# Two filler matmuls of 512 columns ahead of each product of the node network's chunks

## What is computed

```python
h = maximum(layernorm(x), 0)
# layer 0: edge network, sum over a node's edges, node network
e = relu(concat([edge_attr, h[src], h[dst]]) @ We1 + be1)
e_new = relu(e @ We2 + be2) @ We3 + be3
agg = segment_sum(e_new, dst)
g = relu(concat([h, agg]) @ Wn1 + bn1)
g = relu(g @ Wn2 + bn2)
x = x + g @ Wn3 + bn3
h = maximum(layernorm(x), 0)
# layer 1: attention-like weights over 8 heads, weighted sum, 8 products
x = x + layer1(h, src, dst, edge_weight, var_u, var_c, var_w, var_b)
```

## Time and profile before

| | |
|---|---|
| median of three runs | 2298.4 us |
| the profiled execution, its own time | 2296.56 us |
| its span, first to last instruction | 2294.8 us |
| mean granted TensorE clock, share of full | 0.698 |
| PE busy | 1689.2 us (74%) |
| POOL busy | 1626.8 us (71%) |
| DVE busy | 1346.8 us (59%) |
| ACT busy | 848.5 us (37%) |

### The profile page before, as it was taken

How to read it: one execution, slowest core, us unless ns; L and a number is a source line. 1 busy time by engine, 2 the same in 40 slices (tenths; PEclk the granted TensorE clock), 3 DMA queues, 4 the chain that set the end, 5 groups by cost and what they waited for, 6 DMA issues and landing times.

```text
span 2294.8 us, 54235 instructions
## 1 busy us (share of the span) xinstructions
PE 1689.2 (74%) x9941; PEld 1179.9 (51%) x9941; DVE 1346.8 (59%) x5883; ACT 848.5 (37%) x2528; POOL 1626.8 (71%) x1700
## 2 busy tenths in 40 slices
PE   4798999999899988999946656656556565655565
PEld 3455555555555555555435545544445454444454
DVE  6344443434444444344247777777777777777776
ACT  1333333333333333333224444444344434343432
POOL 3777777777777777777437777777777777777773
PEclk7789988989999899898655555555555555555555
DMA  2544444444444444444133333333333333333332
GB/s 75 122 100 102 93 97 96 103 92 101 101 98 96 95 101 99 93 100 97 37 92 99 98 97 97 95 97 94 98 95 97 95 96 96 97 95 96 96 96 60
DMA packets 353333, 216.99 MB, mean 95 GB/s; under 512 B 284830, under 2 KB 325881, under 8 KB 353056
## 3 DMA queue, kind: packets, MB, share of 16 engines
q0 software_dynamic: 66800, 113.26, 21.5%
q1 hardware_dynamic: 284822, 102.20, 18.6%
q10 hardware_dynamic: 1684, 1.24, 0.2%
HBM read 209.80 MB, written 6.69 MB: 94 GB/s over the span
## 4 chain that ended last, share of the span: by engine, by line
issue 24%; DVE 23%; PE 19%; POOL 15%; DVEq 9%; DMA 6%; ACT 3%; POOLq 0%; SPq 0%; ACTq 0%
POOL X L602 15%; DVEq L1246 6%; DMA X<-table_src,slot_s 4%; PE bank L1408 4%; DVE EQW L1187 3%; PE bank L1391 3%; PE bank L1417 3%; ACT EX L831 2%; DVE EX L1227 2%; PE bank L1399 2%; DVE r L1219 2%; DVE r L1210 2%; DVE L L1205 2%; DVE r L1214 2%; DVE r L1223 2%
## 5 line engine op out<-in xcount | busy, mean ns | idle before, releaser
L610 POOL DMA_INDIRECT G<-table_node_and_list,slot_s x825 | 798.6, 968 | 317.0 <-issue 250.7
L602 POOL DMA_INDIRECT X<-table_src,slot_s x825 | 788.5, 956 | 290.7 <-issue 270.3
L1519 PE MATMUL bank<-Q,G 125*64 125x128 f32 x1650 | 419.8, 427 | 398.6 <-DVE Q L1240 398.6
L1519 PEld LDWEIGHTS bank<-Q,G 125*64 125x64 f32 x1650 | 316.7, 223 | 416.9 <-DVE Q L1240 268.1
L1391 PE MATMUL bank<-filler 128*128 128x384 bf16 x1100 | 380.7, 346 | 2.4 <-issue 2.4
L1045 DVE TENSOR_TENSOR sT<-sT,bank 65x16 f32 x275 | 46.2, 168 | 554.0 <-PE bank L1427 523.0
L831 ACT ACTIVATE EX<-L 125x24 f32<-125x24 f32 x275 | 61.2, 223 | 611.2 <-DVE L L1205 597.8
L1408 PE MATMUL bank<-XT,w_ex 128*64 128x375 f32 x550 | 257.4, 553 | 4.2 <-issue 4.2
L763 ACT COPY XT<-bank 128x375 f32<-128x375 f32 x275 | 129.9, 472 | 328.0 <-PE bank L1399 317.5
L1417 PEld LDWEIGHTS bank<-w,H 65*125 65x125 f32 x1650 | 235.2, 202 | 0.0
L1417 PE MATMUL bank<-w,H 65*125 65x64 f32 x1650 | 224.3, 275 | 0.0
(11 more groups left out here) (168 smaller groups left out, 2270.5 us busy)
## 6 DMA issues: line engine op xcount, KB each, us to landing
KBT<-in_dst SPq DMA_DIRECT2D x550, 70.3 KB
X<-in_edge_attr SPq DMA_DIRECT2D x275, 93.8 KB
HK<-keys SPq DMA_DIRECT2D x275, 93.8 KB
X<-table_src,slot_s POOLq DMA_INDIRECT x825
G<-table_node_and_list,slot_s POOLq DMA_INDIRECT x825
BW<-table_dst_parts SPq DMA_DIRECT2D x275, 6.0 KB
UW<-table_logit_src_parts SPq DMA_DIRECT2D x275, 0.8 KB
table_node_and_list<-sm SPq DMA_DIRECT2D x1, 1562.5 KB
```

Source lines behind the costliest of these rows:

```text
L602: pool.indirect_dma_start(X[:, j, q, D:2 * D], None, tA, bass.IndirectOffsetOnAxis(ap=slot_s[:, j, q:q + 1], axis=0)).then_inc(gat_a[0][j] ...
L610: pool.indirect_dma_start(G[:, j, q, :], None, tH, bass.IndirectOffsetOnAxis(ap=slot_s[:, j, q:q + 1], axis=0)).then_inc(g_gather[j], 16)
L1519: last = pe.matmul(bank[2 + j % 2][0:D, 0:WM], G[0:P, j, q, 0:D], Q[:, j % 2, q].rearrange("p m n -> p (m n)"), start=(q == 0), stop=(q == ...
```

## The change

`filler` grows from 384 to 512 columns, `fill` gets a column count that stage 0 leaves at 384, and in the node network two fillers of 512 columns stand ahead of each of g1, g2 and x1, behind the waits of that product and in its bank: 7 chunks x 3 kinds x 2 = 42 matmuls.

```diff
-        filler = sb("filler", [128, 384], BF16)
+        filler = sb("filler", [128, 512], BF16)
...
-            def fill(to):
+            def fill(to, n=384):

-                pe.matmul(to[:, 0:384], filler[:, 0:128], filler[:], start=True, stop=True)
+                pe.matmul(to[:, 0:n], filler[:, 0:128], filler[:, 0:n], start=True, stop=True)
...
                     if c >= 2:
                         done_act(pe, ("g1", c - 2))
+                    for _ in range(2):
+                        fill(bank[c % 2], 512)
                     pe.matmul(bank[c % 2][0:D, 0:hi - lo], wn1h[:], hT[:, lo:hi], start=True, stop=False)
...
                     done_act(pe, ("g1", c))
                     if c >= 2:
                         done_act(pe, ("g2", c - 2))
+                    for _ in range(2):
+                        fill(bank[2 + c % 2], 512)
                     pe.matmul(bank[2 + c % 2][0:D, 0:hi - lo], wn2[:], hT[:, lo:hi], start=True, stop=True
...
                     done_act(pe, ("g2", c))
                     if c >= 2:
                         done_dve(pe, ("x1", c - 2))
+                    for _ in range(2):
+                        fill(bank[4 + c % 2], 512)
                     for n, b in enumerate(chunk_blocks(c)):
```

## The result

The changed kernel takes 2316.14 us (median of 8 runs, 2312.04 to 2317.84) beside 2299.03 us before (8 runs): a ratio of 1.0072, 95% interval 1.0057 to 1.0088. It is 17 us slower. The profiled execution took 2317.82 us, 21.3 more than the one of before; 3.4 of these lie ahead of the network, which stage 0 reached at 1108.14 in place of 1104.73, and that is the scatter of stage 0 from run to run (one and the same kernel, profiled twice as e2 and e9, reached the network at 1104.2 and at 1110.3).

The account below looks back on a forecast made before the run. The prediction took the node network, PE bound at half clock, as what the change could affect. Its terms, -4.2 + 0.5 - 0.8 = -4.5 us, led to 2293 us, own range 2286 to 2298, whole range 2285 to 2319.

Parts of the forecast that it names:

- What bounds the kernel: Node network between the edge loops: PE bound at half clock, PE's gains or losses up to the first half's logits reach the end.
- Which clock: Node network: clock falls at about 1106 us, returns about as late as in stage 0, 9.6 us; gain 4.2 us.
- rival A: Clock stays at half through the network, whose products use 65 rows; fillers all cost, 21.3 us, so 2318; chance 0.25.
- A pair: Two fillers ahead of a network product, with its change of weights: 1.05 us at half clock, 0.6 at full.
- The chunk with fillers at full clock: One chunk of the node network, three products with their filler pairs: 5.5 us at full clock.
- the path up to chunk 3: Network's start to third product of chunk 3: 29.1 us at full clock, 53.4 at half with fillers, 37.7 before.
- break-even: Node network: the change neither gains nor loses if full clock returns 19 us after the network's start.
- The lists: List loads ahead of the table write: about 1.7 us later, 5 us of cover, the bound only for gains above 9 us.
- The layer norm of the first half: On DVE behind the third product of chunk 3: takes 7.3 us whatever PE does, so faster PE gains nothing there.
- The other term: Products with w_u behind the network, already partly at full clock: counted 0, bounds -1 to +1 us.
- The fall at the start: Clock falls to half at about 1106 us, as before, when it fell after 1.2 us of the network.
- Rival B: Clock never falls, as the first filler pair follows the gap at once: gain 8.9 us, 2288 to 2289; chance 0.07.

Follow-up runs that it names:

- e2: The changed kernel plus seven 512-column fillers in the idle time ahead of the network: 2289.80 us profiled, four others 2308.43 to 2313.65; ratio to before 1.0065.
- e9: The kernel of e2 unchanged, profiled once more: 2309.16 us.
- e8: The changed kernel with six fillers over 65 rows, in place of two over 128, ahead of each network product: 2349.22 us, ratio to before 1.0229.
- e6: The changed kernel, two fillers kept, with the network's products over 128 rows in place of 65: 2298.16 us, ratio to before 0.9999.
- e4: The kernel before with the network's products over 128 rows in place of 65, no fillers in the network: 2290.00 us, ratio 0.9964.
- e3: The kernel before plus seven 512-column fillers in the idle time ahead of the network, none in the network: 2296.93 us, ratio 0.9997.
- e11: The kernel of e7 with g1's second matmul reading sT in order, not every 25th element (wrong result, same work): 2288.49 us, one execution.
- e7: The kernel before with network products over 128 rows and seven fillers in the idle time ahead, none in the network: 2288.55 us, ratio 0.9965.
- e1: The changed kernel with six 512-column fillers in place of two ahead of each network product: 2311.31 us, ratio to before 1.0058.
- e10: The changed kernel with four fillers per product in place of two, and seven in the idle time ahead of the network: 2300.17 us, ratio to before 1.0022.
- e5: The changed kernel with four fillers in place of two ahead of each network product: 2333.55 us, ratio to before 1.0156.
- e12: The kernel of e7 with the degree products one product earlier, behind the first chunk's g1: 2286.83 us, ratio to before 0.9959.

## Why the prediction failed

**What bounds the kernel: right.** The network is on the chain, PE bound, and what is lost there arrives at the end: 17.7 us from the network's start to the table write, 17 us in the kernel. Both loops and the table's DMA are as they were.

**The step that failed: "Which clock".** The forecast counted on a return to full clock within some 10 us "about as late as in stage 0", because the fillers' share of the time is the same there and here. It stayed at 0.50 for all of the 61.4 us. The forecast took the fillers for the whole of the difference between the two streams. What the rest of the stream is made of differs as well: stage 0's transposes and window sums use 125 rows and its first product 128, beside smaller ones, while the network's products use 65. e8 and e6 show that this decides: six fillers over 65 rows leave the clock down where six over 128 lift it, and the same two fillers come with 1.00 after 6 us once the products use 128 rows. The rival A had named this reason and was given 0.25; it was the case. That the measured time lies inside the stated range is owed to that rival, for which the range was widened, and not to the forecast. The row for it was in the trace of before, read for another purpose: a PE busy for 44.31 of 45.10 us at 0.50 says that these products do not lift the clock even when PE is busy 98% of the time, and stage 0 is no measure for a stream of them. The Trainium skill asks in general for TensorE to be kept busy (TensorE: Matmul & The Clock Gate, "Why this matters for your kernels"); e4 agrees with that for products over 128 rows, e8, busy for 98.40 us at 0.50, does not for 65.

**Sizes at half clock.** A pair cost (9.87 - 7.18) / 3 = 0.90 us, not 1.05. Two thirds of the difference are the 0.30 us per chunk by which the x1 products became shorter: a change of weights, it seems, was already in L1484's 1.87 and was counted twice. Rival A's sum of 21.3 us was 17.7: up to the third product of chunk 3 1159.45 - 1108.14 = 51.3 in place of 37.7, +13.6 (15.8 told), and behind it +4.1 (5.5 told).

**Sizes at full clock.** e2's profiled run shows them. A pair is 1107.49 - 1106.96 = 0.53 us (0.6 told), L1484's kind 0.82 (1.0 told), but L1466 takes 1.79 at full clock (e3, e4) and not 0.89: its stride sets it there (e11), and it is 1.79 at half clock as well. The prediction had taken L1465's distance in the earlier trace rows for all products of 500 columns. The chunk with fillers at full clock is then 6.1 us, not 5.5, and the path up to chunk 3 about 33 us, not 29.1. Even a return after 9.6 us would have gained 1.3 us, (33 + (1 - 33/51.3) x 9.6 = 36.4 against 37.7), and break-even was at 13 us, not 19. So the mechanism was wrong, and the gain it promised was three times too large.

**The lists: right.** The first list load came 1.7 us later after the network's start (13.3 in place of 11.6 us), as told, and cover was ample. In e7 they did become the bound, as the prediction had said for a gain above 9 us: DVE's copies were through 42.6 us after the network's start in place of 55.3, 12.7 us earlier, and the table write came only 11.3 us earlier (44.1 in place of 55.4).

**Behind the network: two terms wrong, without effect on the result.** The layer norm of the first half was taken to last 7.3 us "whatever PE does". In the changed kernel it was 10.7 us from the third product of chunk 3 to DVE's next addition (1159.45 to 1170.11). DVE waits there for ACT's root (L696), and ACT works in the order of its program, in which the last chunk's ReLU (L806) comes first; that ReLU now waited for the slower PE until 1168.18, and the root followed at 1168.35. Before and after, DVE's first instruction behind the root:

```profile
1148.28 0.25 DVE L908 RECIPROCAL st<-st 125x16 f32<-125x16 f32 x1 [0.38 <-ACT st L696]
1168.67 0.25 DVE L908 RECIPROCAL st<-st 125x16 f32<-125x16 f32 x1 [3.77 <-ACT st L696]
```

It cost nothing, since PE was busy with the network until about 1172 anyway. The other term is L1493, counted as 0 with 1 us either way. Its 32 products for the first half took 4.7 us before and 4.9 after, but 6.9 in e3 and e4 and 4.0 in e7, by the clock that they got. PE alone, e4 and then e7:

```profile
1143.20:1150.10 6.90, 6.89 (x32) 0.50 0.21 48
1141.10:1145.10 4.00, 3.98 (x32) 0.90 0.27 59
```

In both PE had waited 3.8 us for DVE and then run the same transposes. So the clock behind the network scatters, from one execution to the next or with something not found, and it moves the table write by up to 3 us: it is why the profiled runs of e3 and e4 show less at the table write than in the network.

**The fall at the start: right.** It came 1.5 us after the network's start, where 1.2 us was forecast. Rival B did not happen; e2 had to fill the gap for it.

## What to carry over

Before fillers are added to lift TensorE's clock, look at what the stream they join consists of: the granted clock of a stretch in which that stream keeps PE fully busy says what it does by itself. Widening a short contraction with zero weights costs no time on TensorE (L1467 takes the same 0.89 us with 65 and 128 rows) and did here, without a single added matmul, what 42 fillers did not. (The data of the added rows were ones or zeros, and only 128 rows were tried.) And price full clock per instruction: what a strided read sets gains nothing by it. Last, a wait on another engine can grow when one's own engine slows down, since that engine works in order too.

## What was not expected of the hardware

- The number of rows in the contraction counts towards the clock, for bfloat16 fillers (e1 against e8) and for float32 products (the changed kernel against e6).
- The response is a step with memory: four fillers hold full clock, to judge by the times, in nine runs of ten (e10, 2300 us) and do not regain it (e5, 2334 us). Two hold it, to judge by the times, in one run of six (e2, e9), and the fall of e9 came 19 us into a fully busy stretch.
- A float32 matmul of 500 columns whose moving operand takes every 25th element takes 1.79 us at both clocks, against 0.84 read in order at full clock. The Trainium skill (SBUF — State Buffer, the paragraph on cachelines in "Door 1: The DMA port swizzle") says that a read pays a penalty when it goes to a new 16-byte line each time; the 1.79 against 0.84 agrees with it at full clock. At half clock L1465 and L1466 differ only by 1.67 against 1.79.
- The clock can rise right behind float32 transposes. Rows of PE alone in the kernel before: the transposes L1328 fill most of the first stretch, and the second is at 1.00. It does not always: in e3 and e4 the same 16 transposes ran at 0.50, and so did all of the 32 products behind them. The page on TensorE says of transposes that the full clock does not engage for them (the Trainium skill, TensorE: Matmul & The Clock Gate, "Part 4: PE-mode transpose"); the row says otherwise for this execution.

```profile
1150.30:1153.70 3.40, 3.40 (x17) 0.50 0.00 0
1153.70:1157.10 3.40, 2.74 (x25) 1.00 0.00 0
```

- Open: in the kernels with 128 rows stage 1 takes about 3 us longer from its first gather to the end: 1115.6 to 1116.6 in the profiles of e4, e6, e7, e11 and e12, and 1112.1 to 1113.8 in those of the nine others, before's (1112.9) among them. No experiment was made on that; it takes back part of what these kernels gain in the network.
